# Macaron block with a two-expert FFN on one core: the register addresses of the middle slots' weights are summed side by side ahead of each stage's products, as byte addresses

## What is computed

```python
def ffn(x):                       # E = 2 experts, FF = 1024, tokens go to one expert each
    probs = softmax(x @ gate_w.T); sel = argmax(probs); top_w = probs[sel]
    h = silu(x @ w_gate[e].T) * (x @ w_up[e].T)     # for each expert e
    return (h @ w_down[e].T) * (onehot(sel) * top_w)

def attention(x):                 # 16 heads of 16, causal, rms norm in front, residual inside
    xn = rms_norm(x); q, k, v = xn @ Wq, xn @ Wk, xn @ Wv
    return softmax(mask(q @ k.T / 16)) @ v @ Wo + x

x = x + 0.5 * ffn(layernorm(x))
x = x + attention(layernorm(x))
x = x + 0.5 * ffn(layernorm(x))
```

## Time and profile before

| | |
|---|---|
| median of 3 runs | 1240.27 us (1239.09 to 1241.29) |
| profiled execution | 1229.72 us, of which the span from first to last instruction is 1227.9 us |
| mean granted TensorE clock | 0.967 of full speed |
| busy share of the span | PE 88%, DVE 71%, ACT 61%, POOL 47% |
| matmuls | 14214 |

### The profile page before, as it was taken

The page is one execution under the profiler, slowest core; times in us unless marked ns, Lnnn a source line. Parts: engine busy times, 40 slices in busy tenths (PEclk is TensorE's granted clock), DMA queues, the critical chain, the costliest instruction groups (busy, mean ns, idle before and its releaser), DMA issues. The chain is left out here.

```text
span 1227.9 us, 38522 instructions
## 1 busy us (share of the span) xinstructions
PE 1079.0 (88%) x14214; PEld 926.1 (75%) x14214; DVE 871.7 (71%) x1790; ACT 746.8 (61%) x1289; POOL 576.4 (47%) x694
## 2 busy tenths in 40 slices
PE   2687889988989999889989899998999999898894
PEld 1576778767878887778877678877877878787774
DVE  6743747697777886867788867878777798874421
ACT  4532525675667766766667657776766776675321
POOL 3447543345542454635255535335463264645543
PEclk9889899998989999999999899999999999999998
DMA  9103241213211122122222151011321112211212
GB/s 322 63 28 87 74 102 46 76 41 97 58 53 37 46 68 71 38 69 77 63 72 84 41 118 46 29 45 59 89 80 46 40 47 74 73 51 49 58 41 48
DMA packets 108508, 82.97 MB, mean 68 GB/s; under 512 B 57072, under 2 KB 102384, under 8 KB 108336
## 3 DMA queue, kind: packets, MB, share of 16 engines
q1 hardware_dynamic: 90864, 53.49, 15.9%
q0 software_dynamic: 6528, 17.05, 4.5%
q10 hardware_dynamic: 10944, 9.97, 2.4%
HBM read 37.26 MB, written 33.89 MB: 58 GB/s over the span
## 5 line engine op out<-in xcount | busy, mean ns | idle before, releaser
L717 POOL TENSOR_TENSOR h_lo<-hid,h_hi 128x256 bf16<-128x256 f32 x304 | 221.0, 747 | 448.4 <-ACT h_hi L789 448.1
L860 ACT ACTIVATE area<-ps_w,s_scale 128x512 f32<-128x512 f32 x320 | 219.3, 685 | 215.5 <-PE ps_w L1130 88.0
L1083 DVE TENSOR_TENSOR area<-area 128x512 f16<-128x512 f32 x256 | 215.2, 841 | 11.6 <-ACT area L861 9.9
L1227 PE MATMUL ps_g<-x_t,w 128*128 128x128 f16 x1096 | 209.9, 226 | 12.4 <-DMA x_t<-x_sorted 5.3
L861 ACT ACTIVATE area<-ps_w,s_scale 128x512 f16<-128x512 f32 x320 | 217.6, 680 | 0.0
L1229 PE MATMUL ps_g<-x_t,w 128*128 128x128 f16 x1096 | 210.2, 226 | 0.4 <-issue 0.4
L1228 PE MATMUL ps_g<-x_t,w 128*128 128x128 f16 x1096 | 209.2, 225 | 0.4 <-issue 0.3
L1227 PE MATMUL ps_u<-x_t,w 128*128 128x128 f16 x1096 | 205.8, 222 | 3.7 <-issue 3.5
L1229 PE MATMUL ps_u<-x_t,w 128*128 128x128 f16 x1096 | 205.9, 222 | 1.1 <-issue 1.0
L1228 PE MATMUL ps_u<-x_t,w 128*128 128x128 f16 x1096 | 204.5, 220 | 0.1
L1248 PE MATMUL ps_y<-wd,h_hi 128*128 (+1 forms) x608 | 168.8, 278 | 13.2 <-POOL h_lo L717 7.9
(11 more groups left out here) (180 smaller groups left out, 2706.9 us busy)
## 6 DMA issues: line engine op xcount, KB each, us to landing
y_sorted<-ys ACTq DMA_DIRECT2D x76, 128.0 KB
qk_scratch<-area SPq DMA_DIRECT2D x32, 256.0 KB
qt<-qk_scratch SPq DMA_DIRECT2D x128, 64.0 KB, 2.6
kt<-qk_scratch SPq DMA_DIRECT2D x128, 64.0 KB, 2.6
x_buf<-x SPq DMA_DIRECT2D x8, 512.0 KB, 4.1
out<-x_buf SPq DMA_DIRECT2D x7, 512.0 KB, 2.9
x_sorted<-x_buf SPq DMA_DIRECT2D x18, 132.0 KB, 4.9
area<-w_down SPq DMA_DIRECT2D x4, 512.0 KB, 13.1
```

The lines of the kernel that those rows point to most:

```text
L717: pool.tensor_tensor(h_lo[:, u % 2, c], hid[:, u % 2, c], h_hi[:, u % 2, c], ALU.subtract).then_inc(h_lo_done, 1)
L860: act.activation(p_f32[:, f % 3], ps[:], ACT.Exp, scale=s_scale[:])
L1083: dve.tensor_tensor(p_lo[:, f % 4], p_f32[:, f % 3], p_hi[:, f % 4], ALU.subtract).then_inc(lo_done, 1)
L1227: pe.matmul(cols, w_hi, x_hi, start=kb == 0 and f == 0, stop=False, skip_group_check=True)
```

## The change

The byte offset of the middle slot's expert is worked out once per slot in two registers, one for `w16` and one for `wd16`, with the tensors' base addresses already in them (`W_BASE`, `WD_BASE`). A new function `address` makes a register of its own for each weight slice with a single sum. The slice is then taken from a byte view of the tensor (`w8`, `wd8`) at register minus base, so that nothing is left for the build to multiply or add. All addresses of a gate/up stage (8) and of a down stage (4) are made ahead of the stage's first matmul. Matmuls, their operands and order, waits, and the other engines' work stay as they are.

```diff
+            WD_BASE = 8320 + 2 * E * WE
+            W_BASE = 8320 + 2 * (P - 1)
+            numbers = count_up()
+
+            def address(first, offset, base, last):
+                reg = pe.alloc_register(f"w_at{next(numbers)}")
+                pe.reg_add(reg, first, offset)
+                return pe.snap(reg, donate=True, min_val=base, max_val=base + last, guaranteed_mod_val=0, out_of_modulus=2)
+
+            w8, wd8 = w16[:].bitcast(U8), wd16[:].bitcast(U8)
...
-                return w16[:, bass.ds(expert[n, s] + at, P)]
+                return w8[:, bass.ds(address(expert[n, s][0], 2 * at, W_BASE, 2 * E * WE - 2 * P) - W_BASE, 2 * P)].bitcast(F16)
...
-                return wd16[:, bass.ds(expert[n, s] // 2 + at, D)]
+                return wd8[:, bass.ds(address(expert[n, s][1], 2 * at, WD_BASE, 2 * E * DE - 2 * D) - WD_BASE, 2 * D)].bitcast(F16)
...
-                        expert[n, s] = pe.snap((P * s + MAX_COUNT - count[n]) // MAX_COUNT * WE, min_val=0, max_val=WE)
+                        second = (P * s + MAX_COUNT - count[n]) // MAX_COUNT
+                        expert[n, s] = [pe.snap(second * step + base, min_val=base, max_val=base + step)
+                                        for step, base in ((2 * WE, W_BASE), (2 * DE, WD_BASE))]
...
-                    for f in range(QF):
+                    parts = [[gate_up(u, kind, part, kb, q * QF + f) for part in range(2)] for f in range(QF)]
+                    for f, (w_hi, w_lo) in enumerate(parts):
                         cols = ps[:, f * P:(f + 1) * P]
-                        w_hi = gate_up(u, kind, 0, kb, q * QF + f)
                         pe.matmul(cols, w_hi, x_hi, start=kb == 0 and f == 0, stop=False, skip_group_check=True)
                         pe.matmul(cols, w_hi, x_lo, start=False, stop=False, skip_group_check=True)
-                        ins = pe.matmul(cols, gate_up(u, kind, 1, kb, q * QF + f), x_hi, start=False,
+                        ins = pe.matmul(cols, w_lo, x_hi, start=False,
...
-                    for f in (2 * part, 2 * part + 1):
+
+                    parts = [[down(u, k, q * QF + f) for k in range(2)] for f in (2 * part, 2 * part + 1)]
+                    for f, (wd_hi, wd_lo) in zip((2 * part, 2 * part + 1), parts):
                         cols = slice(f * P, (f + 1) * P)
-                        wd_hi, wd_lo = (down(u, k, q * QF + f) for k in range(2))
```

More of the change, by code:

```diff
@@ L1 @@
 from contextlib import ExitStack
+from itertools import count as count_up
 import concourse.bass as bass
@@ L8 @@
 BF16 = mybir.dt.bfloat16
+U8 = mybir.dt.uint8
 F16 = mybir.dt.float16
```

## The result

| | before | changed |
|---|---|---|
| median of the runs | 1239.68 us (1233.54 to 1241.29, 4 runs) | 1220.73 us (1219.21 to 1223.13, 4 runs) |
| ratio | | 0.9874, 95% interval 0.9836 to 0.9912 |
| the profiled execution, and its span | 1229.7 us, 1227.9 us | 1219.21 us, 1217.5 us |

The changed kernel is faster by 1.3%. By the ratio that is 15.6 us of 1239.68, by the medians 19. Two executions of the kernel before in a later set of runs took 2591 and 3559 us; they are left out of all medians and ratios here.

The account below looks back on a forecast made before the run. The prediction took PE's sequencer, computing weight addresses between matmuls, as the limit of middle slots. Its terms, -6.1 - 6 - 1 - 0.5 + 1 = -12.6 us, bring the median from 1240.3 to 1227.7 us; own range 1221 to 1234, wider 1215 to 1238.

Parts of the forecast that it names:

- (b): Between 128 and 1120 us: some 13 us of delayed matmul starts, nearly half of it gained, -6 us.
- (d): Between 1137 and 1160 us: PE works on fillers while the last batch's scatter path has its own length; -0.5 us.
- the heads: Starts of gate/up stages: two register instructions ahead of the first matmul, 22 with empty queue, 2.7 us at most; +1 us.
- What bounds a middle slot: Middle slots: PE's sequencer, 0.124 us per register instruction, needs 0.99 us for a gate/up stage against the array's 0.67.
- (a): Last pass, 1178.95 to 1204.98 us: five units fall from 26.03 to 19.95 us, all of it gained, -6.1 us.
- (c): Before 128 us: 3.8 us of lost starts mostly end in waits for split weights, x_t and first norm; -1 us.
- Nothing: Rival: the 82 ns come from addressing weights through a register, or the array's pace, not computing it; 1240 us, chance 0.08.
- Absorbed: Rival: only the last pass gains, and less than whole, -2 to -6 us, 1234 to 1238 us; chance 0.13.
- Everything back: Rival: lost starts in (b) to (d) lie mostly on chains through PE and come back; 1214 to 1221 us, chance 0.15.
- Slower: Rival: sums bared at stage heads cost 0.124 us each; with 208 bare stages the kernel takes 1253 us; chance 0.07.

Follow-up runs that it names:

- one_register: Against the kernel before: middle slots read one weight slice for all products at the slot's register address, no sum per address; 1209.14 us, ratio 0.9847.
- in_place: Against the kernel before: each address one sum on an absolute byte address, still made right ahead of its product; 1221.21 us, ratio 0.9948.
- old_form_ahead: Against the changed kernel: addresses still made ahead of the stage, but with three operations each as before the change; 1219.26 us, ratio 0.9926 to the kernel before.
- five_ops_ahead: Against the changed kernel: five dependent operations per address instead of one sum, all ahead of the stage; 1264.23 us, ratio 1.0212 to the kernel before.
- last_pass_only: The change in the last pass alone, the kernel before's address form in the other eleven; 1230.05 us, ratio 0.9929 to the kernel before.
- before_again: The kernel before, unchanged, run again for a second profile; median 1240.74 us in that set of runs.
- next_ahead: Against the changed kernel: a stage's addresses made after the first block of the FFN stage before it, within one slot; 1222.36 us, ratio 0.9857 to the kernel before.
- all_but_last: The change in eleven passes, the kernel before's address form in the last; 1226.97 us, ratio 0.9933 to the kernel before.

## Why the prediction held, step by step

The changed kernel's 1220.73 us lies in the forecast's range of 1215 to 1238, 7 us below the 1227.7 itself and just outside that case's own 1221 to 1234. The changed kernel gained 15.6 to 16.8 us by its three ratios where 12.6 were forecast. So 3 of the 7 us are a gain larger than forecast, from terms (b), (d) and the heads. The other 4 are spread between runs: the median of four runs was 1239.68 for the kernel before, and medians of the changed one differ as much (1220.73, 1219.77 and 1224.54).

**What bounds a middle slot.** Right, and shown from three sides. Without sums the operand in a register costs nothing (one_register); with the sums in place but shorter and a tenth fewer instructions, the unit shrinks by what these save (in_place, 4.52 us); with the sums ahead it shrinks to the array's 3.99 us even at four packed instructions a stage (old_form_ahead). The 0.124 us of the forecast is 46 ns of record and some 78 ns around it. Side by side it is 59 ns around a record of 74 (0.133 us), so the greater part of the 78 goes with the instruction wherever it stands, and what counts is how many there are.

One step of the account was wrong without harm to this forecast. I took a down stage as bound by the array, 4 x 0.99 + 2 x 0.65 = 5.3 us, while the sequencer set the pace through the whole unit, 40 instructions at 0.124 us and some longer steps. For the kernel before the two sums come out alike, by luck. For the experiments they do not: 4.8, 4.4 and 6.2 us a unit were expected of in_place, old_form_ahead and five_ops_ahead from the first sum, and 4.52, 3.99 and 5.21 measured.

**(a), last pass.** Forecast 26.03 to 19.95, measured 19.96. It came out exact because a unit at the array's pace was in the trace already, in the last slot, and no other engine was busy for more than a third of the 26.03 us. The ratio of last_pass_only, 8.8 us (5.2 to 12.4), agrees.

**(b), the middle.** The mechanism was right and the size too small: 6 was forecast, and 5.5 to 10.7 measured, with 10.4 in the pair from one set of runs. Single profiles of the changed kernel differ by 5 us there, so the size is known no better than that. The stretch's gross size of 13 was well sized, since PE's busy time fell by 10 to 12 us. (Added up again, the 649 held pairs give 19.4 us over 56 ns and not 21.4, 9.1 of it in the middle; scaled by the last pass the middle still holds about 14.) The term that was mis-sized is the share lost in waits. I took more than half; between 1.4 and 6.3 us came back as idle time, in the pair of one set 1.7 of 12.1, and the larger figures hold part of the stalls. The waits that I had listed were not where it went: those for `p_lo` (`ps_v`) and `row_min` hardly grew. The one for `h_lo`, within the FFN units themselves, may have: with its part under "issue" it is 12.5 and 15.9 us in the two profiles of before, and 16.2, 17.8 and 19.3 in the three of the changed kernel, a step no larger than that between the two of before. The other waits seem to move forward with PE, since their releasers work on PE's earlier products. That is argued from the idle times; no run tested a single wait.

**(c), before 128 us.** 1 was forecast, and the matmul of 128.0 us started at 127.4 in the changed kernel, 126.9 and 127.0 in its other profiles, against 127.7 in before_again: 0.3 to 0.8 us. It was small, as forecast; PE is idle a third of that stretch.

**(d), 1120 to 1160.** 0.5 was forecast. The same matmuls took 40.1 us in both profiles of before and 37.9, 38.4 and 38.3 in the changed kernel, a gain of 2. The wait that I leaned on is still there and as long as before, on SP's queue (in total, times, longest):

```profile
SPq L548 <- DMA x_sorted<-xs_rows,place: 39.6, 1, 39.6
```

It is 0.4 us shorter than in the earlier trace rows. I had counted the whole stretch as fixed by that transfer because one wait in it was long. That the path to the scatter itself begins with PE's products, which now come earlier, would explain the 2 us, but no run shows it. From 1160 to the last pass's units the same matmuls took 18.8 and 18.2 us before, and 17.4, 20.8 and 21.3 in the changed kernel, of which the two long ones had 3.4 and 6.8 us at the lower clock; nothing is read from it.

**The cost of the heads.** Forecast 22 x 0.124 = 2.7 us at most. The 22 stages of that forecast and the 33 in an expectation above were not counted by one rule. By the rule given with old_form_ahead the two profiles of the kernel before have 53 and 54 bare gate/up heads and 38 and 39 bare down heads, and the three of the changed kernel 26, 22 and 26, and 14, 13 and 14. So there are fewer, as the forecast guessed. From the first of two register instructions to the load it is 0.23 us where nothing runs beside them, but in 18 to 23 of them the first of the two still runs under earlier products, and some 0.1 us is bare, as at a head of the kernel before. One head in the changed kernel (start, duration, instruction, idle time before):

```profile
329.32 0.19 PEld L1117 LDWEIGHTS ps_w<-wa_hi,xt_lo 128*128 128x128 f32 x1
329.75 0.10 PEld L1245 LDWEIGHTS ps_g<-x_t,w 128*128 x1 [0.24 <-issue]
329.78 0.10 PEld L1246 LDWEIGHTS ps_g<-x_t,w 128*128 x1
329.83 0.10 PEld L1247 LDWEIGHTS ps_g<-x_t,w 128*128 x1
```

So the +1 us of this term did not come: half as many heads are bare, at about the same price each. That is one of the reasons why the gain was larger than forecast. next_ahead, which takes away most of the down heads, is 2 us faster in its median, unproven.

**The rules weighed.** The Trainium skill's page "TensorE: Matmul & The Clock Gate", section "Back-to-back issue gap", gives about 81 ns per matmul at 128 columns. The traces do not agree: units with register addresses take 3.99 us for all their products, at 0.05 to 0.06 us a product within a stage. The Trainium skill's page "Advanced Engine Details and Errata", section "Sequencer Loop", says that other engine instructions can be read and queued while microcode runs. In this kernel register instructions between matmuls do hold the array up (0.25 us for a block of three); old_form_ahead shows when they do not, with enough products queued in front of them.

**The rivals.** "Nothing" fell with one_register. "Absorbed" fell with all_but_last. "Everything back" was the other end of one scale, and the truth lies beyond the middle of it towards that end. "Slower" is a real mechanism (five_ops_ahead) that the change stays clear of, with 22 to 26 bare gate/up heads and two register instructions at each.

**What stays open.** What the stalls of 0.25 to 1.4 us inside gate/up stages are, which cost 7 to 11 us in three sets of runs and nothing in the fourth; how much of the 10 us between old_form_ahead and one_register are heads; whether next_ahead is better than the change; and whether the gain of the middle stretch is nearer 5 or 10 us, since the clock's lower level and the stalls fall anew in each execution.

## What to carry to other kernels

If matmuls of 128 columns stand in a loop with addresses from registers, look at the spacing of weight loads, not at PE's busy share, which counted the stall as work here. Count register instructions per stage rather than their operations: gathered ahead of a stage they are packed, and they run under the products already queued, as long as the sequencer's whole work for a unit stays below the array's. Add up the sequencer's time over the unit and not stage by stage, since a lead won in one stage is spent in the next. To size a gain spread over a long stretch, compare two profiles of the same kernel first; here the kernel before moved by 7 us between two, about 4 of it in low-clock products inside gate/up stages and 2.6 in stalls.

## What the runs showed of the hardware

- A packed register instruction of PE takes 42 ns for two sums, 60 for four and 74 for six, some 7 to 9 ns for each further one. A single operation takes 32 ns.
- Between two matmuls about 78 ns come on top of each such record (periods of 0.124 us at 46 ns and 0.112 at 32). Between register instructions that stand side by side it is about 59 ns (0.133 us at 74 ns, in old_form_ahead and five_ops_ahead; 0.138 in the changed kernel). Seven packed ones took 0.91 us up to the load, four took 0.52.
- A matmul's operand addressed by a register costs nothing that these runs can show (0.9847 against 0.9841, and 19.95 us for the same five units).
- Matmuls of 128 columns with a weight load each start every 56 ns in gate/up stages, with fixed and with register addresses (3.99 us a unit, both).
- Stalls of 0.25 to 1.4 us between matmuls, most with no register instruction and no wait between them, came 10 to 18 times in each of nine profiles and once in all in four others (6.6 to 11.2 us against 0.2).
- The granted clock of the same kernel had a mean of 0.967 and 0.962 in two profiles, and of 0.959, 0.953 and 0.958 in three of the changed one, whose spans were 1217.5, 1217.4 and 1223.1 us. Its lower level falls at other places each time, and the mean alone did not order the times.
